# A fused cross-attention kernel: value products of a step's last tile moved into one block with the row sums and the next step's first values, and those of tiles 2 and 3 put together

## What is computed

```python
x = (hidden_states - mu) * jax.lax.rsqrt(var + LN_EPS) * ln_gamma + ln_beta
Q = _split_heads(x @ Wq.T)                                # B=2, S=512, HIDDEN=1024, 32 heads of 32
K = _split_heads(memory_keys)                             # context, (2, 1024, 1024)
V = _split_heads(memory_values)                           # the same context
scores = jnp.einsum('bhsd,bhtd->bhst', Q, K) * scale
scores = jnp.where(mask, scores, -jnp.inf)
probs = jax.nn.softmax(scores, axis=-1)
attn = jnp.einsum('bhst,bhtd->bhsd', probs, V)
out = attn.transpose(0, 2, 1, 3).reshape(B, S, HIDDEN) @ Wout.T
return residual + out
```

## Time and profile before

| | us |
|---|---|
| median of 3 runs | 697.75 (695.89 to 698.48) |
| the profiled execution, time | 697.61 |
| its span in the trace | 695.8 |
| a step, from one bias transpose (367.96) to the next (396.27) | 28.31 |

### The profile page before, as it was taken

One profiled execution on the slowest core, in us unless ns is written; L12 is line 12 of the kernel. 1 busy time (PEld: TensorE's weight loads), 2 busy tenths in 40 slices (PEclk: granted clock), 3 DMA queues, 4 the chain that ended last, 5 costly groups with the idle time before them and its releaser, 6 DMA issues.

```text
span 695.8 us, 10773 instructions
## 1 busy us (share of the span) xinstructions
PE 663.1 (95%) x3537; PEld 390.2 (56%) x3537; DVE 453.0 (65%) x494; ACT 337.5 (49%) x614; POOL 392.3 (56%) x107
## 2 busy tenths in 40 slices
PE   2799999989999999999999999999999999999998
PEld 2677787844444444454544444444444444678886
DVE  6763434059878788787887877878878575633231
ACT  3652121255675666566656667566566665400000
POOL 1000000048498797887977979779788798800000
PEclk9999999999999999999999999999999999999999
DMA  9712010255515426154262452533605113033131
GB/s 344 193 37 82 31 31 1 62 122 130 144 55 137 97 74 155 48 132 113 61 159 59 109 123 76 136 78 90 149 20 136 62 36 118 31 121 122 60 121 60
DMA packets 40286, 68.10 MB, mean 98 GB/s; under 512 B 5668, under 2 KB 22694, under 8 KB 40238
## 3 DMA queue, kind: packets, MB, share of 16 engines
q1 hardware_dynamic: 39956, 67.25, 35.4%
q10 hardware_dynamic: 292, 0.40, 0.2%
HBM read 25.18 MB, written 4.19 MB: 42 GB/s over the span
## 4 chain that ended last, share of the span: by engine, by line
PE 88%; DVE 4%; ACT 3%; DMA 2%; issue 2%; SPq 1%; POOL 0%; ACTq 0%; DVEq 0%; POOLq 0%
PE SX L968 19%; PE MX L946 18%; PE PV L984 17%; PE MX L1102 13%; PE MX L974 6%; PE PV L909 6%; PE SX L909 5%; PE MX L886 2%; PE MX L956 1%; PE SX L901 1%; ACT PR L636 1%; DMA PR<-in_x 1%; ACT PR L546 1%; PE MX L880 1%; DVE R L717 1%
## 5 line engine op out<-in xcount | busy, mean ns | idle before, releaser
L758 DVE TENSOR_REDUCE mx<-MX 128x1 f32<-128x1024 f32 x256 | 302.6, 1214 | 81.8 <-PE MX L946 78.8
L636 ACT ACTIVATE PR<-SX 128x512 f32<-128x512 f32 x512 | 267.7, 601 | 142.5 <-PE SX L968 137.4
L507 POOL TENSOR_TENSOR acc<-acc,PR 128x2048 f32<-128x2048 f32 x64 | 293.7, 4590 | 8.7 <-POOL acc L507 7.6
L507 POOL TENSOR_TENSOR acc<-PR 128x2048 f32<-128x2048 f32 x16 | 73.4, 4590 | 206.2 <-ACT PR L636 206.2
L968 PE MATMUL SX<-R 99*128 99x512 f32 x512 | 177.2, 426 | 3.7 <-ACT PR L636 2.8
L946 PE MATMUL MX<-R 97*128 97x512 f32 x512 | 165.8, 407 | 4.5 <-DMA R<-QT 1.5
L968 PEld LDWEIGHTS SX<-R 99*128 99x128 f32 x512 | 88.7, 190 | 100.2 <-ACT PR L636 77.3
L984 PE MATMUL PV<-PR,C 128*32 128x512 f32 x1024 | 136.4, 605 | 0.1
L946 PEld LDWEIGHTS MX<-R 97*128 97x128 f32 x512 | 90.3, 189 | 54.2 <-DVE mx L758 34.8
L984 PEld LDWEIGHTS PV<-PR,C 128*32 128x32 f32 x1024 | 20.1, 108 | 46.0 <-issue 26.2
L855 DVE TENSOR_TENSOR PR<-PR,MX 128x512 f32<-128x512 f32 x16 | 10.9, 686 | 53.3 <-PE MX L1102 51.7
(11 more groups left out here) (84 smaller groups left out, 476.4 us busy)
## 6 DMA issues: line engine op xcount, KB each, us to landing
R<-KTh SPq DMA_DIRECT2D x60, 256.0 KB, 4.3
PR<-in_x SPq DMA_DIRECT2D x16, 512.0 KB, 4.1
C<-in_ctx SPq DMA_DIRECT2D x16, 512.0 KB, 3.5
R<-QT SPq DMA_DIRECT2D x62, 128.0 KB, 2.5
R<-KTl SPq DMA_DIRECT2D x60, 128.0 KB, 3.9
acc<-in_L_xattn_Wq SPq DMA_DIRECT2D x8, 512.0 KB, 3.7
C<-in_L_xattn_Wout SPq DMA_DIRECT2D x8, 512.0 KB, 3.7
R<-QT SPq DMA_DIRECT2D x62, 64.0 KB, 2.1
```

Source lines behind the costliest of these rows:

```text
L507: nc.gpsimd.tensor_tensor(acc[:, :, :], a, PR[:, tt % RING, :, :], ALU.add).then_inc(pool_used, 1)
L636: nc.scalar.activation(PR[:, tt % RING, h, :], SX[bank(HPG * tt + h)][:, :], ACT.Exp, scale=SCALE).then_inc(exp_done, 1)
L758: nc.vector.tensor_reduce(mx[:, u % 2, i:i + 1], MX[par][:, :], mybir.AxisListType.X, ALU.max, negate=True).then_inc(mx_freed, 1)
```

## The change

In slots 0 and 1 the values of tile 7 of the step before move from slot 0 to slot 1, ahead of the row sums; the row sums become an early item, and values of tile 0 follow them. In slot 3 no values stand any more; those of tiles 2 and 3 both stand in slot 4, in one row. `pv_copy` moves from slot 0 to slot 1 on ScalarE. The items are placed anew to go with it: slot 0 has two instead of three, slots 3 and 4 two each (before three and two), slot 5 three, and in slot 6 `maxima(2, 0)` and `bias(1)` both stand after the values. The sequence of maxima is the same; maximum 5 now comes after `keys` and `sums` rather than ahead of them.

```diff
 STEP = [
-    (maxima(1, 4), maxima(1, 5), keys(2)),
-    ([], sums(-1), maxima(1, 6)),
+    ([], maxima(1, 4), keys(2)),
+    (sums(-1), maxima(1, 5), maxima(1, 6)),
     (maxima(1, 7), [], maxima(1, 8)),
...
-    (maxima(2, 0), bias(1), maxima(2, 1)),
+    ([], maxima(2, 0) + bias(1), maxima(2, 1)),
     (maxima(2, 2), [], maxima(2, 3)),
 ]
+
+
+VALUES_AT = {2: (1,), 4: (2, 3), 5: (4,), 6: (5,), 7: (6,)}
...
-            items[tt] = ([], sums(-1) if tt == 1 else [], wout(o))
+            items[tt] = (sums(-1) if tt == 1 else [], [], wout(o))
...
-                    if tt == 0 and not first:
+                    if tt == 1 and not first:
                         pv_copy(n - 1)
...
+                    if tt == 1 and not first:
+                        values(n - 1, u + RING - 1, TT - 1)
                     for item in early:
                         mx_item(*item)
-                    if tt >= 1:
-                        values(n, u, tt - 1)
-                    elif not first:
-                        values(n - 1, u + RING - 1, TT - 1)
+                    if tt == 1:
+                        values(n, u, 0)
+                    for old in VALUES_AT.get(tt, ()):
+                        values(n, u, old)
```

More of the change, by code:

```diff
@@ L117 @@
 STEP = [
-    (maxima(1, 4), maxima(1, 5), keys(2)),
-    ([], sums(-1), maxima(1, 6)),
+    ([], maxima(1, 4), keys(2)),
+    (sums(-1), maxima(1, 5), maxima(1, 6)),
     (maxima(1, 7), [], maxima(1, 8)),
-    (maxima(1, 9), maxima(1, 10), maxima(1, 11)),
-    (maxima(1, 12), [], maxima(1, 13)),
-    (maxima(1, 14), [], maxima(1, 15)),
-    (maxima(2, 0), bias(1), maxima(2, 1)),
+    ([], maxima(1, 9), maxima(1, 10)),
+    ([], maxima(1, 11), maxima(1, 12)),
+    (maxima(1, 13), maxima(1, 14), maxima(1, 15)),
+    ([], maxima(2, 0) + bias(1), maxima(2, 1)),
     (maxima(2, 2), [], maxima(2, 3)),
 ]
+VALUES_AT = {2: (1,), 4: (2, 3), 5: (4,), 6: (5,), 7: (6,)}
 def is_first(n):
```

## The result

The changed kernel takes 713.39 us (median of 4 runs, 711.97 to 717.68), the kernel before 698.12 beside it (695.89 to 701.07): a ratio of 1.0242, with an interval from 1.0198 to 1.0286. The forecast was 707.3 with a range from 702.0 to 712.0. It is slower, as forecast, but by 15.3 us and not by 9.7. The profiled execution has a span of 715.8 us against 695.8, so 20.0 us are to be accounted for.

A forecast was written before the change was run, and what follows sets the result against it. The prediction took TensorE's queue to bound the kernel. Steps 1 to 13 at +0.82 us each gave +10.7, less 0.4, 0.3 and 0.3 elsewhere: +9.7 on 697.61, so 707.3 us, range 702.0 to 712.0.

The forecast's parts named there:

- The view on TensorE's queue: Whole kernel: a step lasts as long as TensorE's queue, with TensorE busy for 95% of the span.
- the price of slot 6: Slot 6, between maxima 0 and 1: 2.14 us needed, 1.12 left, so TensorE waits 1.02 us in each step.
- The regular step: Steps 1 to 13: savings and waits sum to +0.82 us, so a step goes from 28.31 to 29.13.
- Each join: At the sums and at tiles 2 and 3: one values entry and exit fewer saves 0.33 us, 0.66 a step.
- The first rival: No slot 6 wait; a round through GpSimd, ScalarE and tile 0's values sets steps of 28.5 to 28.65; 700.5 us; chance 0.07.
- Rival 2: Regular steps: neither slot 6's wait nor GpSimd's round binds, joins are earned in full; 686 us, faster; chance 0.03.
- the small waits: Maxima 5 to 7, 8 to 10, 11 to 13, 3 to keys: TensorE waits for VectorE, 0.54 us a step together.
- The sum on the regular part: Steps 1 to 13 add 10.7 us; steps 14, 15 and the loop's head take off 0.4, 0.3, 0.3: +9.7.
- At the loop's head, three times: Loop's head: an existing wait already covers the 0.12 us wait at the keys, three times, giving -0.3 us.
- The third rival: The clock falls in the new waits; in each step that adds 22 us, giving 729 us; chance 0.03.
- price of a fall: TensorE's clock behind a wait: 3.4 us at half speed lose 1.7 us.
- Step 0, "taken as nothing": Step 0 keeps its table and joins tiles 2 and 3: between -0.3 and +0.3 us, counted as zero.

The follow-up runs named there:

- e9: Kernel before with only slot 6 edited: maximum 0 moved behind tile 5's values, directly ahead of the bias transpose; 710.54 us, ratio 1.0179.
- e1: Changed kernel with slot 6 as before: maximum 0 ahead of tile 5's values, bias transpose behind them; 706.85 us, ratio 1.0123.
- e5: Kernel before with only the slots 0 and 1 half of the change: tile 7's values, sums and tile 0's values in one row; 705.11 us, ratio 1.0108.
- e7: Changed kernel with slot 6 as before, ScalarE's loop written out and step 0's values in their old slots; 698.14 us, ratio 1.0004.
- e10: e7 with the second of GpSimd's five additions over two heads instead of four, so its result differs; 695.27 us, ratio 0.9970.
- e2: Changed kernel with ScalarE's loop over steps 1 to 12 written out, other engines keeping their loops; 709.77 us, ratio 1.0148.
- e4: Kernel before with ScalarE's loop written out; 694.95 us in 10 runs, ratio 0.9964.
- e3: Changed kernel with the values of step 0 in the slots they had before; 712.99 us, ratio 1.0206.

## Why the prediction was right, and where it failed

**The view on TensorE's queue, and the price of slot 6: right.** The forecast had 2.14 us needed and 1.02 waited. Measured are 2.05 between the starts, and a pair that lasts 0.56 (380.93 to 381.49) in place of 0.46, which together is 2.15; e9 alone makes the step 1.03 longer. TensorE did not go around the waiting maximum. That agrees with the second of the two pages that the prediction weighed, the section Engine vs sequencer instructions of PSUM — Partial Sum Buffer in the Trainium skill: products keep program order.

**The regular step: right, and not by luck.** Forecast 29.13, measured 29.15 (29.10 to 29.20). The terms can be read one by one from the changed kernel's timeline, start against start as the prediction did it, in one step (379.45 to 408.60). Each small wait is what its scores and its item take over the usual:

```
term                                   forecast   measured
wait in slot 6                            1.02       1.0
maximum 5 to 7  (394.03)                  0.15       0.17
maximum 8 to 10 (398.21)                  0.13       0.17
maximum 11 to 13 (403.25)                 0.14       0.17
maximum 3 to the keys (386.06)            0.12       0.12
tile 5's values behind scores (407.04)    0.09       0.08
maximum 10 to 12 (402.23)                -0.17      -0.17
```

Each join saves 0.14 inside the run (1.86 in place of 1.00 and 1.00) and the rest of the 0.33 in the products ahead of it and behind. With -0.66 the measured column makes +0.88, and the step is 0.85 longer.

**The first rival: its mechanism is real.** It stood at 28.5 to 28.65, and wherever slot 6's wait was away, in e1, e5 and e7, the step was 28.55 to 28.60. It was right not to be the forecast, since the longer wait covers it. Rival 2, the joins earned in full, is out: with both slot 6 and the circle relieved (e10) the step is 28.37. It needed more than the two bounds to go: the small waits and the one at maximum 0 eat the joins.

**The sum on the regular part: right in size.** From the table of the stretches: 8.5, the heads' regular share of 1.7, and the ends make 10.3, against 9.7 forecast. In it step 14 is about half a microsecond of luck, the wait for a DMA that only the kernel before had there. There are two heads of ScalarE's loop inside the steps, not three, and they got nothing back.

**The step that failed: "At the loop's head, three times, a wait that is there already covers the 0.12: -0.3".** The prediction took the 0.6 by which the step with the head was longer before as a fixed wait, and let a small new wait vanish in it. In fact the pause of ScalarE was some 2 us (1.95 of "issue"), and the work that covered it was the values block and maximum 5, the two items that the change moves away from that place. The timeline of before showed both: "issue" 1.95 on ScalarE, and on TensorE the 1.57 us of work between the scores. It was not read at that place. Taking the cover away turned 0.18 into 2.13. e2 and e4 show that it is the branch: with the loop written out the extra is gone in both kernels. It costs 6.5 us in the profiled execution, (33.02 - 29.15) + (32.95 - 29.15) less the 1.2 of before.

**The clock: a condition read off wrongly.** The third rival got 0.03 since "the new waits are shorter than both" of the waits seen before, 1.44 and 1.68. At the heads they were not: 2.13 and 2.08. Having missed that wait, the prediction had no place for a fall. Its price of a fall, 1.7 for 3.4 us at 1.2 GHz, is a little high: the heads of e1, e3 and e5 give 1.5. In the regular steps the clock stayed at 1.00 behind 0.74 of idle time, as said.

**Step 0, "taken as nothing".** Its wait for the split keys grew by 1.00, the time of tile 2's values that had covered it, and 6.8 us at half the clock followed, in each of the three kernels that have it. The term should have been +1.0 for the wait, outside the -0.3 to +0.3 given, and with the clock it was +3.65. It is the same mistake as at the head: the place was costed by what TensorE does there, not by what it waits for. The interval of e3 is too wide to show how much of it reaches the median.

Together: 9.7 forecast, 0.6 of small slips, 6.5 at the heads, 3.65 in step 0, less 0.45 ahead of it, make the 20.0 of the profiled execution. The median is 4.3 us under that execution. The runs differ in their mean clock (0.987 in the profiled one, up to 0.994 in another), so falls of the clock, which not every run need have at the same places, are likely the difference; there is no trace of the other runs to show it.

## What to carry to other kernels

When work is moved from one place to another, ask first what it covered at the old place, above all at a loop's branch: an engine's pause of 2 us there can show as 0.2 us of waiting, and the whole of it comes out when the cover leaves. With two buffers, write down the distance from start to start that a reuse needs (here 2.05) and check it wherever the order changes; a block that looks like pure overhead may be what fills it. And edits whose stalls cover each other don't add up: 0.30, 0.10 and 1.03 us a step alone were 0.85 together.

## What the runs showed of the hardware

- ScalarE's loop over steps costs it some 2 us at each branch (1.89 to 2.25 of idle time with nothing to wait for, at the sixteen heads of the eight kernels that have the loop); written out, a step with the head is as long as the others, 28.28 in place of 28.92.
- The granted clock fell to 1.2 GHz around single waits of TensorE of 1.5 to 2.1 us, but not around all of them, and their length does not separate the two cases. At one and the same wait for a DMA in step 0 it fell behind 1.48, 1.56, 1.57 and 2.00, and held behind nine waits of 1.12 to 1.50. At the heads it fell around 1.83, 1.85, 1.94, 2.08 and 2.13 (e3, e5, e1 and the changed kernel twice), and held behind 1.77, 1.79 and 1.90 (e1, e3, e5). In e3 the fall began at 293.53, before the wait ended at 293.80. A fall of 3.4 us cost 1.5.
- A pair of maxima's products, its reduction over 128x1024 on VectorE and the way back to the buffer's next use take 2.05 us from start to start: 0.77 until VectorE begins, 1.22 for the reduction, 0.06 until the load.
- A run of values blocks between other products costs 0.33 more than its blocks do inside a run: two blocks in one row take 1.86 in place of 1.00 and 1.00, the rest is in the products ahead and behind.
- GpSimd's addition over half the columns takes 2.39 against 4.60 us: nearly in proportion.
